# Scan layer: the products dt·x·B of state groups 10 and 12 move to GpSimd, and x is added by TensorE

## What is computed

```python
def step(h, inp):
    x_t, dt_t, B_t, C_t = inp
    dA = jnp.exp(dt_t[:, :, None] * A)
    h = dA * h + dt_t[:, :, None] * B_t[:, None, :] * x_t[:, :, None]
    y = jnp.einsum('bds,bs->bd', h, C_t)
    return (h, y)
...
y = yT.transpose(1, 0, 2) + xc * D_skip
y = y * jax.nn.silu(z)
return y @ W_out
```

## Time and profile before

| what | value |
|---|---|
| median of 3 runs | 3429.43 us (3426.34 to 3430.45) |
| profiled execution | 3435.36 us, its span 3433.5 us |
| busy in the span: TensorE, VectorE, GpSimd, ScalarE | 2695.1, 2517.5, 1988.5, 1903.8 us |
| largest groups of the scan layer: GpSimd line 451, VectorE lines 425 and 420 | 1205.3, 1170.5, 620.5 us, 512 of each |
| granted TensorE clock, mean of the span | 0.919 of full speed |

### The profile page before, as it was taken

How to read it: one execution, slowest core, us unless ns; L and a number is a source line. 1 busy time by engine, 2 the same in 40 slices (tenths; PEclk the granted TensorE clock), 3 DMA queues, 4 the chain that set the end, 5 groups by cost and what they waited for, 6 DMA issues and landing times.

```text
span 3433.5 us, 39492 instructions
## 1 busy us (share of the span) xinstructions
PE 2695.1 (78%) x12378; PEld 807.8 (24%) x12378; DVE 2517.5 (73%) x2227; ACT 1903.8 (55%) x2344; POOL 1988.5 (58%) x1216
## 2 busy tenths in 40 slices
PE   5867878668877686547888888888888888888886
PEld 2222222323122231112222222222222222222221
DVE  4534554435545344236999999999999999999998
ACT  2513456224545133327767677777767677777672
POOL 2423223423134242026787878788888888888886
PEclk9978999879989698768999999999999999999999
DMA  3657423667206575555767575757576757676764
GB/s 134 192 179 244 140 69 107 203 204 216 93 32 204 179 246 151 126 111 126 172 142 176 141 177 141 180 141 179 139 178 140 180 140 175 144 174 147 169 153 113
DMA packets 276064, 536.66 MB, mean 156 GB/s; under 512 B 59448, under 2 KB 170496, under 8 KB 275056
## 3 DMA queue, kind: packets, MB, share of 16 engines
q1 hardware_dynamic: 241440, 450.04, 50.3%
q0 software_dynamic: 17568, 59.00, 6.3%
q10 hardware_dynamic: 16944, 26.17, 3.1%
HBM read 396.55 MB, written 138.54 MB: 156 GB/s over the span
## 4 chain that ended last, share of the span: by engine, by line
PE 19%; issue 17%; DVE 16%; POOL 1%; ACT 1%; DVEq 0%; DMA 0%; POOLq 0%; SPq 0%; ACTq 0%
DVE m_pb L420 11%; PE m_pb L270 6%; PE m_py L253 6%; DVE m_hs L425 5%; PE m_misc L218 3%; PE m_misc L237 2%; PE m_misc L224 1%; DVE m_gated L407 1%; PE m_py L249 1%; POOL m_hs L451 1%; DVEq L424 0%; DMA m_dtb<-dt_rows 0%; DVE m_fin L435 0%; POOL m_dt L467 0%; POOL m_sp_v L460 0%
## 5 line engine op out<-in xcount | busy, mean ns | idle before, releaser
L451 POOL TENSOR_TENSOR m_hs<-m_hs,m_cs 128x1024 f32<-128x1024 f32 x512 | 1205.3, 2359 | 344.8 <-DVE m_hs L425 344.8
L425 DVE TENSOR_TENSOR_SCAN m_hs<-m_da,m_pb 128x1024 f32<-128x1024 f32 x512 | 1170.5, 2286 | 31.3 <-ACT m_da L377 6.2
L270 PE MATMUL m_pb<-m_dtx,late 64*128 64x512 f32 x2048 | 597.9, 649 | 217.8 <-DVE m_hs L425 217.1
L377 ACT ACTIVATE m_da<-m_dtb,m_a_neg 128x1020 f32<-128x1020 f32 x512 | 579.5, 1143 | 289.0 <-DMA m_dtb<-dt_rows 219.5
L420 DVE TENSOR_TENSOR m_pb<-m_pb,m_bs 128x1024 f32<-128x1024 f32 x512 | 620.5, 1212 | 34.1 <-PE m_pb L270 33.3
L253 PE MATMUL m_py<-m_hs,late 128*64 128x512 f32 x2048 | 566.1, 632 | 61.1 <-POOL m_hs L451 61.1
L1372 POOL TENSOR_TENSOR t_xc<-t_xc,big 128x512 f32<-128x512 f32 x96 | 119.3, 1267 | 409.8 <-DVE big L1278 409.8
L1148 ACT ACTIVATE t_sq<-t_bank 128x512 f32<-128x512 f32 x192 | 105.5, 595 | 399.8 <-PE t_bank L1013 399.6
L270 PEld LDWEIGHTS m_pb<-m_dtx,late 64*128 64x128 f32 x2048 | 168.3, 188 | 615.4 <-DVE m_hs L425 535.0
L1160 ACT ACTIVATE t_gate<-t_bank,t_small 128x512 f32<-128x512 f32 x192 | 121.6, 683 | 299.4 <-PE t_bank L957 295.4
L948 PE MATMUL t_bank<-late,t_lwin 128*128 128x256 f32 x816 | 236.5, 427 | 60.6 <-ACT big L1163 35.4
(11 more groups left out here) (152 smaller groups left out, 3699.8 us busy)
## 6 DMA issues: line engine op xcount, KB each, us to landing
m_dtb<-dt_rows SPq DMA_DIRECT2D x512, 512.0 KB, 6.1
late<-right_factor POOLq DMA_DIRECT2D x102, 512.0 KB, 6.1
right_factor<-t_tile SPq DMA_DIRECT2D x192, 256.0 KB, 4.0
t_tile<-band_out SPq DMA_DIRECT2D x183, 256.0 KB, 4.2
band_out<-t_vwin SPq DMA_DIRECT2D x48, 496.0 KB
band_out<-t_vwin SPq DMA_DIRECT2D x48, 480.0 KB
dt_rows<-m_dt ACTq DMA_DIRECT2D x64, 256.0 KB, 3.2
t_xc<-in_x_cm SPq DMA_DIRECT2D x4, 2048.0 KB, 14.6
```

What stands on the lines that cost most here:

```text
L270: m = nc.tensor.matmul(pb[s % 2][:, half(n)], spread[rows, dg, :], dtx[par][rows, half(q)], start=True, stop=True)
L377: nc.scalar.activation(da[:, s % DA_RING, :, 1:T], dtb[s % DTB_RING][:, :].rearrange("p (r t) -> p r t", t=T)[:, :, 1:T], ACT.Exp, scale=a ...
L425: nc.vector.tensor_tensor_scan(hs[:, s % H_RING, :], da[:, s % DA_RING, :, :].rearrange("p r t -> p (r t)"), pb[s % 2][:, :], 0.0, ALU.mul ...
L451: nc.gpsimd.tensor_tensor(hs[:, s % H_RING, :], hs[:, s % H_RING, :], cs[q][:, :], ALU.mult).then_inc(hc_ready, 1)
```

## The change

Of the 16 groups of a chunk, 10 and 12 (`APART`) take another way to `h`. TensorE spreads their dt·x early, behind its steps 3 and 4, into `misc`; ScalarE copies it into the SBUF tiles `ub`, behind its steps 4 and 5; GpSimd multiplies `ub` by B behind its groups 5 and 6 (ops u0, u1); and ScalarE copies the product back into `pb`, just ahead of its decay of group 12 and of group 14, once the scan before has released the buffer. VectorE then only scans these two.

VectorE's `fin` goes too: x is added by TensorE, as a product with an identity matrix `eye` into `py[1]` ahead of the product with `w_out`, reading x in place with a step of 64 elements, and ScalarE copies `py[1]` into `fin` behind its step 9. In the tables, TensorE's cq1 moves from step 4 to 5 and dt from 5 to 6, ScalarE's cq1 from 5 to 6. One more weight, `eye` (64 KB), is loaded before the layer. The results are the same sums, `x` now taken through TensorE.

Cut to what matters:

```diff
+    APART = (10, 12)
+    INLINE = [s for s in range(S) if s not in APART]
...
+        ub = [sb(f"ub{i}", [P, W]) for i in range(len(APART))]
...
-        USE = {"x": 0, "bq1": 1, "cq1": 2, "dt": 3, "z": 4, "bq0": 5, "cq0": 6}
+        USE = {"x": 0, "bq1": 1, "u0": 2, "u1": 3, "cq1": 4, "dt": 5, "z": 6, "bq0": 7, "cq0": 8}
+        OWN_USE = ("bq1", "u0", "u1", "cq1")
...
+        def inline(k, s):
+            return len(INLINE) * k + INLINE.index(s) + 1
...
-            "tensor": {0: [(PRE, "x")], 2: [(OWN, "bq1")], 4: [(OWN, "cq1")], 5: [(PRE, "dt")], 8: [(PRE, "z")],
-                       7: [(POST, "out")], 9: [(PRE, "bq0")], 11: [(PRE, "cq0")]},
-            "scalar": {1: [(PRE, "silu_x")], 3: [(OWN, "bq1")], 5: [(OWN, "cq1")],
-                       6: [(PRE, "dt0"), (PRE, "dt1"), (PRE, "sp_abs")], 7: [(PRE, "sp_exp"), (PRE, "sp_ln"), (PRE, "sp_sum")],
-                       8: [(PRE, "sp_back"), (PRE, "sp_relu")], 9: [(PRE, "silu_z")], 10: [(PRE, "bq0")], 12: [(PRE, "cq0")],
+            "tensor": {0: [(PRE, "x")], 2: [(OWN, "bq1")], 3: [(OWN, "u0")], 4: [(OWN, "u1")], 5: [(OWN, "cq1")], 6: [(PRE, "dt")],
+                       7: [(POST, "out")], 8: [(PRE, "z")], 9: [(PRE, "bq0")], 11: [(PRE, "cq0")]},
+            "scalar": {1: [(PRE, "silu_x")], 3: [(OWN, "bq1")], 4: [(OWN, "u0")], 5: [(OWN, "u1")],
+                       6: [(OWN, "cq1"), (PRE, "dt0"), (PRE, "dt1"), (PRE, "sp_abs")],
+                       7: [(PRE, "sp_exp"), (PRE, "sp_ln"), (PRE, "sp_sum")], 8: [(PRE, "sp_back"), (PRE, "sp_relu")],
+                       9: [(POST, "fin"), (PRE, "silu_z")], 10: [(PRE, "bq0")], 12: [(PRE, "cq0")],
                        13: [(NEXT2, "xg0")], 14: [(POST, "store"), (PRE, "dt_rows")], 15: [(NEXT2, "xg1")]},
-            "vector": {4: [(POST, "gate1")], 8: [(POST, "out")], 11: [(OWN, "gate0")]},
-            "gpsimd": {7: [(PRE, "loss0"), (PRE, "log0")], 8: [(PRE, "dt0"), (PRE, "loss1")],
+            "vector": {4: [(POST, "gate1")], 11: [(OWN, "gate0")]},
+            "gpsimd": {5: [(OWN, "u0")], 6: [(OWN, "u1")], 7: [(PRE, "loss0"), (PRE, "log0")], 8: [(PRE, "dt0"), (PRE, "loss1")],
                        9: [(PRE, "log1"), (PRE, "dt1")], 10: [(PRE, "dtx0")], 11: [(PRE, "dtx1")]},
...
+                    elif op in U_OPS:
+                        apart = APART[int(op[1])]
+                        q = apart // DG
+                        pe.wait_ge(dtx_ready, 2 * k + q + 1)
+                        for n in range(2):
+                            rows = slice(D * n, D * n + D)
+                            pe.wait_ge(misc_used[n], use(k, op))
+                            nc.tensor.matmul(misc[n][:, :], spread[rows, apart % DG, :], dtx[par][rows, half(q)],
+                                             start=True, stop=True).then_inc(misc_ready[n], 1)
...
-                    if not (first and s < 2):
-                        pe.wait_ge(h_ready, g - 1)
-                    for n in range(2):
-                        rows = slice(D * n, D * n + D)
-                        m = nc.tensor.matmul(pb[s % 2][:, half(n)], spread[rows, dg, :], dtx[par][rows, half(q)],
-                                             start=True, stop=True)
-                    m.then_inc(b_ready, 1)
+                    if s in INLINE:
+                        if not (first and s < 2):
+                            pe.wait_ge(h_ready, g - 1)
+                        for n in range(2):
+                            rows = slice(D * n, D * n + D)
+                            m = nc.tensor.matmul(pb[s % 2][:, half(n)], spread[rows, dg, :], dtx[par][rows, half(q)],
+                                                 start=True, stop=True)
+                        m.then_inc(b_ready, 1)
...
+                    nc.tensor.matmul(py[1][:, :], eye[:, :], xm[:, :, bass.ds(SUB * k, SUB)].rearrange("p t n -> p n t"),
+                                     start=True, stop=False, skip_group_check=True)
                     for q in range(2):
                         m = nc.tensor.matmul(py[1][D * q:D * q + D, :], w_out[:, :], gated[:, half(q)],
-                                             start=True, stop=True, skip_group_check=True)
+                                             start=False, stop=(q == 1), skip_group_check=True)
...
+                        i = int(op[1])
+                        for n in range(2):
+                            a.wait_ge(misc_ready[n], use(k, op) + 1)
+                            nc.scalar.copy(ub[i][:, half(n)], misc[n][:, :]).then_inc(misc_used[n], 1)
...
-                            a.wait_ge(busy, S * k if q else S * k - DG)
+                            a.wait_ge(busy, per * k if q else per * k - late)
...
+                    if s - 1 in APART:
+                        i = APART.index(s - 1)
+                        a.wait_ge(u_made[i], k + 1)
+                        a.wait_ge(h_ready, S * k + s - 2)
+                        nc.scalar.copy(pb[(s - 1) % 2][:, :], ub[i][:, :]).then_inc(u_back[i], 1)
...
+                    if op == "fin":
+                        a.wait_ge(o_ready, k + 1)
+                        if not early(k, 1):
+                            a.wait_ge(stored, 16 * G * k)
+                        nc.scalar.copy(fin[:, :], py[1][:, :]).then_inc(fin_done, 1)
+                        return
...
-                    v.wait_ge(b_ready, g + 1)
-                    nc.vector.tensor_tensor(pb[s % 2][:, :], pb[s % 2][:, :], bs[q][:, :], ALU.mult).then_inc(u_done, 1)
-                    v.wait_ge(u_done, g + 1)
+                    if s in INLINE:
+                        v.wait_ge(b_ready, inline(k, s))
+                        nc.vector.tensor_tensor(pb[s % 2][:, :], pb[s % 2][:, :], bs[q][:, :], ALU.mult).then_inc(u_done, 1)
+                        v.wait_ge(u_done, inline(k, s))
+                    else:
+                        v.wait_ge(u_back[APART.index(s)], k + 1)
...
-                        v.wait_ge(o_ready, k + 1)
-                        if not early(k, 1):
-                            v.wait_ge(stored, 16 * G * k)
-                        nc.vector.tensor_tensor(fin[:, :].rearrange("p (n t) -> p n t", n=SUB),
-                                                py[1][:, :].rearrange("p (n t) -> p n t", n=SUB),
-                                                xm[:, :, bass.ds(SUB * k, SUB)].rearrange("p t n -> p n t"),
-                                                ALU.add).then_inc(fin_done, 1)
...
+                    if op[:-1] == "u":
+                        j = APART[q] // DG
+                        for n in range(2):
+                            g_.wait_ge(misc_used[n], use(k, op) + 1)
+                        nc.gpsimd.tensor_tensor(ub[q][:, :], ub[q][:, :], bs[j][:, :], ALU.mult).then_inc(u_made[q], 1)
...
+    a["eye"] = np.eye(P, dtype=np.float32)
...
```

More of the change, by code:

```diff
@@ L48, in mamba_layer @@
         gn_bias = sb("gn_bias", [P, 1])
-        (avg, w_in, conv_w, w_z, wx_dt, w_dt, w_bc, w_out, w_skip, vecs, a_log, spread, gather) = (t for t, _ in shared.weights)
+        (avg, w_in, conv_w, w_z, wx_dt, w_dt, w_bc, w_out, w_skip, vecs, a_log, spread, gather, eye) = (t for t, _ in shared.weights)
         w_conv = sb("w_conv", [P, TAPS // 2, P])
@@ L136, in mamba_layer @@
         dt_stored = [sem(f"dt_stored{i}") for i in range(2)]
+        u_made, u_back = ([sem(f"{n}{i}") for i in range(len(APART))] for n in ("u_made", "u_back"))
         dtb_loaded = [sem(f"dtb_loaded{i}") for i in range(DTB_RING)]
@@ L149, in use @@
                 return FIRST_USE[name]
-            body = k if name in ("bq1", "cq1") else k - 1
+            body = k if name in OWN_USE else k - 1
             if isinstance(k, int) and body == CHUNKS - 1:
-                return len(FIRST_USE) + len(USE) * body + ("bq1", "cq1").index(name)
+                return len(FIRST_USE) + len(USE) * body + OWN_USE.index(name)
             return len(FIRST_USE) + len(USE) * body + USE[name]
+        U_OPS = tuple(f"u{i}" for i in range(len(APART)))
+        def inline(k, s):
+            return len(INLINE) * k + INLINE.index(s) + 1
         def stores_of(k, par):
@@ L361, in pre @@
                         nc.scalar.activation(sp_x[:, :], sp_x[:, :], ACT.Relu).then_inc(sp_relu, 1)
+                    elif op in U_OPS:
+                        i = int(op[1])
+                        for n in range(2):
+                            a.wait_ge(misc_ready[n], use(k, op) + 1)
+                            nc.scalar.copy(ub[i][:, half(n)], misc[n][:, :]).then_inc(misc_used[n], 1)
                     else:
-                        dst, busy = ((bs, u_done), (cs, hc_ready))["bc".index(op[0])]
+                        dst, busy, per, late = ((bs, u_done, len(INLINE), len([s for s in INLINE if s >= DG])), (cs, hc_ready, S, DG))["bc".index(op[0])]
                         q = int(op[2])
                         if not early(k, 1):
-                            a.wait_ge(busy, S * k if q else S * k - DG)
```

(14 more changed lines are left out.)

2 lines of the change are left out of this document (1 added, 1 removed).

## The result

The changed kernel takes 3515.28 us (median of 4 runs, 3512.04 to 3521.12), the kernel before 3429.26: 1.0251 of its time, with a 95% interval of 1.0237 to 1.0264. It is slower by 86 us, where 58 were forecast. The profiled execution took 3513.15 us. Its span, from the first instruction to the last, is 3511.0 us, where 3491.9 were forecast. Lines are those of the changed kernel: VectorE's product is L460, its scan L467, GpSimd's groups L484, its new products L495, ScalarE's copy back L414, TensorE's spread L291, sum L273, x L229, bq0 L257.

What follows compares the result with a forecast made beforehand. VectorE was taken to set the 57.61 us period before, GpSimd's chain after the change. Terms 2.4+29x2.0+0.2-3.4+1.0+0.2=58.4 us more gave a median of 3488 us, 1.7% slower, range 3432 to 3520.

Steps and rivals of the forecast that it cites:

- Taken from VectorE: VectorE, per chunk: two products and fin removed, 3.43 us less; period 54.18 us if nothing else ends later.
- GpSimd's chain: GpSimd, groups 5 to 13: group 7 2.39 us later, 0.39 us room, next chunk's group 1 product 2.0 later; period 59.6.
- From there to the next E(5) nothing changes: From next chunk's group 1 product to E(5), VectorE's next start after scanning group 5: stays 18.0 us.
- ScalarE's copy back: ScalarE, group 10: copied back 17.3 us after VectorE's scan of group 5; VectorE waits 3.6 us; this chain's period 57.8.
- The rows through DRAM: Rows issued behind GpSimd's dt1, 2.4 us later; of 4.0 us room some 2 stay, so no cost.
- TensorE's identity product: TensorE, step 7 ahead of w_out: 0.93 us, or 1.9 if the strided read hurts; 2.6 us room, no period cost.
- Half clock: Rival: TensorE slows at group 13's sum and x, next group 1 product 1 to 1.5 us later; 3518 to 3533 us; 0.11.
- VectorE as the bound: Rival: GpSimd's idle time takes in its new products, each chunk saves 3.43 us; 3321 us; 0.11 for this or near it.

Runs made afterwards that it cites:

- e4: Changed kernel with each scan's waits reordered (own product last) and GpSimd's two new products behind groups 3 and 4 instead of 5 and 6; 3474.98 us, 1.0141.
- e9: e7 with bq0 and cq0 later on TensorE and ScalarE, and ScalarE's xg1 one step earlier; 3425.38 us, 0.9988 of the kernel before.
- e5: Kernel before with only the fin part of the change (TensorE's identity product, ScalarE's copy); 3418.83 us, 0.9968.
- e6: Changed kernel with counts of spreads and products going up by 16 a chunk, so waits around a product compare with one value; 3489.74 us, 1.0180.
- e3: Changed kernel with each scan's waits reordered (own product last) and ScalarE's copies back right behind the same group's decay; 3503.14 us, 1.0215.
- e7: e6 with GpSimd's two products behind groups 3 and 4 and ScalarE's copies back early; 3461.15 us, 1.0104 of the kernel before.
- e8: e7 with TensorE's product x cut in halves, behind steps 0 and 1; 3438.70 us, 1.0035 of the kernel before.
- e2: Changed kernel with each scan's waits reordered (own product last) and GpSimd's two new products left out; 3476.73 us, 1.0144.
- e10: e9 with x in two halves and GpSimd's dtx1 behind group 14 instead of 11; 3404.10 us, 0.9918 of the kernel before.
- e11: e10 with TensorE's cq0 one step earlier and ScalarE's copy of it behind step 14; 3357.25 us, 0.9782 of the kernel before.

## Why the prediction was right, and what it mis-sized

The direction and the mechanism were right, the size was 28 us short.

- *Taken from VectorE.* Right: 56.8 - 53.5 = 3.3 us busy time less per chunk.
- *GpSimd's chain.* Right to 0.1 us where it ends. Group 7 starts 9.48 us after E(5) instead of 7.05, +2.43 for a forecast of 2.39; the product of 1' follows at 41.63 for 41.6. e4 and e9 show that it is the place of the two products that costs, e5 that the room was 0.4 us. The wait before the product of 1' is 1.1 us and not the forecast 1.8, because the register steps behind the copy back, 0.16 us each, fill a part of it; it is 1.4 in e6.
- *From there to the next E(5) nothing changes.* This is the term that was mis-sized: 18.67 us, not 18.0. From the product of 1' to E(5) stand five scans, and against the kernel before they come later behind their products by 0.09, 0.09, 0.15, 0.16 and 0.15 us, because the loop's waits compare with two different counts and the second is worked out between product and scan. It is 0.64 us a chunk; the measured 60.31 - 59.64 = 0.67 over the 28 chunks of the loop make 18.8 us. I had read the change's `inline(k, s)` as bookkeeping. The price could have been found in the trace of before, in the wider gaps of groups 0 to 2 (above, e6). The layer alone, from VectorE's first product in it to the end, grew by 80 us in the profile (1864.1 to 1944.5), where 58 were forecast: 22 short, of which the steps are 19 (from after to e6 the layer shrank by 18.8). Some 3 are left, in chunks that now and then last 0.2 to 0.6 us longer and at the ends. The other 5 or 6 us of the measured 86 lie outside the layer: its first product came 2.9 us earlier in the profile of after, and the profiled execution of before was 6 us above its median, that of after 2 below.
- *ScalarE's copy back.* Right for itself (17.2 for 17.3; 3.69 us of wait in e6 for 3.6), and rightly hidden behind GpSimd's chain. But its second way to VectorE, through silu_z, bq0 and the spread of 11, was not seen. In the changed kernel it costs nothing of its own; in e3 it took the place of the copy back, and it kept most of the gain expected of e7 and e8.
- *The rows through DRAM.* "Nothing" was right for the changed kernel. But what ScalarE has queued behind the decay of 0' waits with it: in e2, e4 and e7 x waited so for xg1, and VectorE stood 0.6 to 1.1 us before the product of 1'.
- *TensorE's identity product.* The upper end of its range, and no cost to the period, as forecast: 1.96 us for the two matmuls. By mean duration:

```profile
L301 PE MATMUL m_py<-big,late 128*128 x2 | 2.0, 1069 | 0.0
```

The other product of that size, line 269, takes 592 ns at the least. The page of the Trainium skill that was weighed (SBUF — State Buffer, "Door 1: The DMA port swizzle") says that reads which cross to a new 16-byte line each time pay a penalty; for TensorE this trace agrees, with 1069 ns against 592. The prediction's 687 ns of ScalarE (line 329) are those of a read from PSUM; the contiguous row from SBUF is line 361, 1040 ns for 1024 elements, and against that 1286 ns for 512 are more, not less.

- *The rivals.* Half clock did not occur between group 13 and 1' (x takes 3.70 us in the changed kernel too). It did elsewhere: in the changed kernel at the spread of group 11 (2.08 us at 2275.93), where VectorE was held by the copy back and it cost nothing, and at group 10 in e9 and e10, where it cost. VectorE as the bound is what e11 comes near to, with the counts and the places of seven pieces of work changed together; to relieve the busiest engine paid only after the chains beside it had been shortened.

## What to carry to other kernels

Before work is taken from the busiest engine, measure by how much each other chain is ahead of it at the point where they meet. Where that was 0.4 us a chunk, savings of 0.95 us (e5) and of 3.4 us (e9) both brought the period from 57.6 to 57.3. Work added to the other engine ahead of that point costs what the idle time before it doesn't take in: here 2.4 of 4.6 us. The remedy is a place, not less work: the two products cost 30 us or more behind groups 5 and 6 and nothing behind 3 and 4. Where a kernel loops over a register, keep the counts of all waits around a hot instruction equal, if need be by counting 2 where a step is left out.
